# Mamba core units of 32 channels by 4 states, with shared tiles of step sizes and inputs, in a fused attention, FFN and Mamba kernel

## What is computed

```
def step(h, inp):
    dt_t, B_t, C_t, u_t = inp
    dA = jnp.exp(dt_t[..., None] * A)
    h = dA * h + (dt_t * u_t)[..., None] * B_t[:, None, :]
    y_t = jnp.einsum('ben,bn->be', h, C_t)
    return (h, y_t)
```

## Time and profile before

| | |
|---|---|
| median of 3 runs | 813.26 us (810.76 to 814.96) |
| the profiled execution | 808.2 us, its span 806.4 us |
| busy: PE, DVE, ACT, POOL | 729.3, 690.0, 613.8, 598.2 us |
| mean granted TensorE clock | 0.976 of full speed |
| DMA | 152.93 MB, q1 at 70.4% of 16 engines' span |

### The profile page before, as it was taken

How to read it: one execution, slowest core, us unless ns; L and a number is a source line. 1 busy time by engine, 2 the same in 40 slices (tenths; PEclk the granted TensorE clock), 3 DMA queues, 4 the chain that set the end, 5 groups by cost and what they waited for, 6 DMA issues and landing times. The chain is left out here.

```text
span 806.4 us, 22760 instructions
## 1 busy us (share of the span) xinstructions
PE 729.3 (90%) x8284; PEld 441.3 (55%) x8284; DVE 690.0 (86%) x1147; ACT 613.8 (76%) x1227; POOL 598.2 (74%) x589
## 2 busy tenths in 40 slices
PE   6989996998789999999899989979998999788888
PEld 5666653644455446556465366546555555354557
DVE  6878146999999999998899899999998989889963
ACT  4767686899779999998699988888669557656423
POOL 3023254878898998879797798889989989898751
PEclk9999998999999999999999999989999999799999
DMA  6000017798879769877768898979798999799940
GB/s 205 3 3 2 2 57 171 204 232 235 200 210 238 198 190 237 231 220 199 188 201 219 216 251 235 254 204 264 222 246 213 237 259 239 211 284 232 229 118 28
DMA packets 83025, 152.93 MB, mean 190 GB/s; under 512 B 9305, under 2 KB 9954, under 8 KB 82914
## 3 DMA queue, kind: packets, MB, share of 16 engines
q1 hardware_dynamic: 82914, 151.48, 70.4%
HBM read 140.43 MB, written 11.01 MB: 188 GB/s over the span
## 5 line engine op out<-in xcount | busy, mean ns | idle before, releaser
L1798 POOL TENSOR_TENSOR d<-d,cr 128x1024 f32<-128x1024 f32 x128 | 300.4, 2355 | 27.0 <-DVE d L1303 17.3
L1620 ACT ACTIVATE ps<-dt,An 128x512 f32<-128x512 f32 x252 | 170.7, 691 | 59.9 <-DVE d L1303 43.1
L1303 DVE TENSOR_TENSOR_SCAN d<-ps,hl,d 128x512 f32<-128x512 f32 x128 | 157.8, 1266 | 4.4 <-ACT ps L1620 2.6
L1303 DVE TENSOR_TENSOR_SCAN d<-ps,d 128x512 f32<-128x512 f32 x128 | 150.5, 1206 | 6.5 <-ACT ps L1620 4.9
L892 PE MATMUL ps<-h,w 128*128 128x512 f16 (+1 forms) x512 | 118.0, 382 | 7.3 <-DVE h L1238 6.7
L1291 DVE TENSOR_TENSOR d<-ps,d 128x512 f32<-128x512 f32 x182 | 117.3, 671 | 5.9 <-DMA d<-dud 5.9
L1785 POOL TENSOR_TENSOR d<-d,br 128x512 f32<-128x512 f32 x70 | 88.8, 1275 | 19.9 <-DMA d<-dud 16.1
L892 PEld LDWEIGHTS ps<-h,w 128*128 128x128 f16 x512 | 47.6, 99 | 80.9 <-DVE h L1238 17.5
L981 PE MATMUL ps<-d,cst 128*32 128x512 f32 x512 | 69.6, 619 | 7.7 <-POOL d L1798 7.2
L1028 PEld LDWEIGHTS ps<-cst 128*128 128x128 f32 x476 | 59.4, 200 | 18.2 <-issue 10.2
L1028 PE MATMUL ps<-cst 128*128 128x128 f32 x476 | 63.4, 287 | 5.3 <-DMA cst<-in_w 5.3
(11 more groups left out here) (183 smaller groups left out, 1368.8 us busy)
## 6 DMA issues: line engine op xcount, KB each, us to landing
d<-dud SPq DMA_DIRECT2D x252, 256.0 KB, 5.1
dt<-dtd SPq DMA_DIRECT2D x252, 256.0 KB, 5.6
dud<-sE SPq DMA_DIRECT2D x16, 256.0 KB, 4.5
dtd<-sR SPq DMA_DIRECT2D x16, 256.0 KB, 3.9
X<-in_x SPq DMA_DIRECT2D x8, 256.0 KB, 6.2
br<-bcd SPq DMA_DIRECT2D x8, 256.0 KB, 3.3
cr<-bcd SPq DMA_DIRECT2D x8, 256.0 KB, 3.7
out<-X SPq DMA_DIRECT2D x3, 512.0 KB, 5.6
```

Of the source, the lines that this page charges most:

```text
L1303: eng.tensor_tensor_scan(d, banks[u % NG][:, :], d, hl[:, r:r + 1] if m % 2 else 0.0, ALU.mult, ALU.add).then_inc(v_sc, 1)
L1620: eng.activation(banks[u % NG][:, :], src[:, :], ACT.Exp, scale=An[:, g:g + 1]).then_inc(s_da, 1)
L1798: eng.tensor_tensor(d, d, CR[m % 2][:, :].unsqueeze(1).to_broadcast((128, n, 512)), ALU.mult).then_inc(p_cm, n)
```

## The change

A unit becomes 32 channels by 4 states. Unit u of block k = u // 4 has the states 4w to 4w + 3 with w = u % 4, and the four units of a block share their 32 channels. One tile of step sizes and one of inputs then serve four units: `dt4_d` and `du4_d` load 32 rows given 4 times, into 2 slots each (`DT`, and a new `DU`). Since B_t and C_t now differ with w, `BR` and `CR` have four tiles each and are no longer doubled: `br_d` may reload tile w after the last drive that reads it, `cr_d` after the last `out_p`. The roles in the drive are turned round: `bp_s` copies the inputs of a block (`DU`) into `PB`, 62 times instead of 8 times `BR`, and `drive_v` multiplies `PB` by `BR[w]` straight into the slot of `D`, for which it waits itself (`t_y`). `drive_p` reads `DU`. POOL drives the units with w = 0; the first two blocks (`SPREAD`), eight units, are spread by PE. `ND` goes from 12 to 10. `PLACES` has new numbers throughout, and PE's warming products (`WARM`) go from 238 to 207.

```diff
-def channels(r):
-
-    return r // 16, r % 4, r % 16 // 4
-
-
-
-DRIVEN_P = [0, 1, 5, 9, 13, 17, 21, 25, 29]
-
-
-FIRST = 4
+SPREAD = 2
+
+
+DRIVEN_P = [0, 4, 8, 12, 16, 20, 24, 28]
 
 
 def driver(u):
 
-    return "v" if u < FIRST or u % NR not in DRIVEN_P else "p"
+    return "v" if u < 4 * SPREAD or u % NR not in DRIVEN_P else "p"
...
 
-        ND = 12
+        ND = 10
         D = sb("d", [128, ND, 512])
...
-        NT = 6
+        NT, NQ = 2, 2
         DT = sb("dt", [128, NT, 512])
-        BR = [sb(f"br{i}", [128, 512]) for i in range(2)]
-        CR = [sb(f"cr{i}", [128, 512]) for i in range(2)]
+        DU = sb("du", [128, NQ, 512])
+        BR, CR = (sb(n, [128, 4, 512]) for n in ("br", "cr"))
...
-                if m >= 2:
-
-                    eng.wait_ge(t_mo, m - 1)
+
+            def states(m, at):
+
+                return bcd[m % 2][at:at + 4, :].unsqueeze(1).to_broadcast((4, 32, 512))
+
+            def br_d(m, w):
+                u = NR * m - 4 + w
                 eng.wait_ge(l_bc, 16 * (m + 1))
-                for i, dst in enumerate((BR[k], CR[k])):
-                    eng.dma_start(dst[:, :], bcd[k][16 * i:16 * i + 16, :].unsqueeze(1).to_broadcast((16, 8, 512))).then_inc(l_br, 16)
+                if m and driver(u) == "v":
+                    eng.wait_ge(v_dr, driven(u + 1, "v"))
+                elif m:
+                    eng.wait_ge(p_dr, driven(u + 1, "p"))
+                eng.dma_start(BR[:, w, :], states(m, 4 * w)).then_inc(l_b[w], 16)
+
+            def cr_d(m, w):
+                eng.wait_ge(l_bc, 16 * (m + 1))
+                if m:
+                    eng.wait_ge(p_cm, NR * m - 4 + w // 2 * 2 + 2)
+                eng.dma_start(CR[:, w, :], states(m, 16 + 4 * w)).then_inc(l_c[w], 16)
...
-            def rows(src, u):
-
-                m, r = u // NR, u % NR
-                eb, q, w = channels(r)
-                e = 128 * eb + 32 * q + 8 * w
-                return src[m % 2][e:e + 8, :].unsqueeze(0).to_broadcast((16, 8, 512))
-
-            def dt8_d(u):
-                if u >= NT + FIRST:
-                    eng.wait_ge(s_da, u - NT + 1)
-                eng.wait_ge(l_dt, 16 * (u // 16 + 1))
-                eng.dma_start(DT[:, u % NT, :], rows(dtd, u)).then_inc(l_t[u % NT], 16)
-
-            def du8_d(u):
-                if u == FIRST:
-
-                    eng.wait_ge(v_set, V_END)
-                if u >= ND:
-                    eng.wait_ge(t_y, (u - ND) // 4 + 1)
-                eng.wait_ge(l_du, 16 * (u // 16 + 1))
-                eng.dma_start(D[:, u % ND, :], rows(dud, u)).then_inc(l_d[u % ND], 16)
+            def rows(src, k):
+
+                m, eb, q = k // 8, k // 4 % 2, k % 4
+                e = 128 * eb + 32 * q
+                return src[m % 2][e:e + 32, :].unsqueeze(0).to_broadcast((4, 32, 512))
+
+            def dt4_d(k):
+                if k >= NT + SPREAD:
+                    eng.wait_ge(s_da, 4 * (k - NT) + 4)
+                eng.wait_ge(l_dt, 16 * (k // 4 + 1))
+                eng.dma_start(DT[:, k % NT, :], rows(dtd, k)).then_inc(l_t[k % NT], 16)
+
+            def du4_d(k):
+                if k >= NQ + SPREAD:
+                    eng.wait_ge(s_bp, k - NQ - SPREAD + 1)
+                    eng.wait_ge(p_dr, driven(4 * (k - NQ) + 4, "p"))
+                eng.wait_ge(l_du, 16 * (k // 4 + 1))
+                eng.dma_start(DU[:, k % NQ, :], rows(dud, k)).then_inc(l_q[k % NQ], 16)
...
+
+                bank = bank_of["bdt", k] = turn((s_da, 4 * k + 4))
                 eng.wait_ge(v_md, 2)
-                q = slice(32 * u, 32 * u + 32)
+                q = slice(32 * k, 32 * k + 32)
...
-                m, eb, w = k // 8, k // 4 % 2, k % 4
-                if w == 0:
+                m, eb, q = k // 8, k // 4 % 2, k % 4
+                if q == 0:
...
-                for q in range(4):
-                    t = eng.matmul(bank[32 * q:32 * q + 32, :], csel[:, 24 - 8 * w:56 - 8 * w], D[:, (4 * k + q) % ND, :],
+                for w in range(4):
+                    t = eng.matmul(bank[32 * q:32 * q + 32, :], spread[:, 0:32], D[:, (4 * k + w) % ND, :],
                                    start=(w == 0), stop=(w == 3))
...
 
                     eng.wait_ge(l_dt, 16 * n)
                 if n == 1:
-                    eng.wait_ge(t_bdt, FIRST)
+                    eng.wait_ge(t_bdt, SPREAD)
                 eng.wait_ge(p_md, 3 * n + 2)
                 eng.scalar_tensor_tensor(sR[:, :], bank_of["md", m, eb][:, :], 0.0, sL[:, :], ALU.max, ALU.add).then_inc(v_md, 1)
 
             def drive_v(u):
-                m = u // NR
-                d = D[:, u % ND, :]
-                if u < FIRST:
+                m, w, k = u // NR, u % 4, u // 4
+                if u < ND:
 
                     eng.wait_ge(v_set, V_END)
-                    eng.wait_ge(l_br, 32)
-                    eng.wait_ge(t_bdu, u + 1)
-                    eng.tensor_tensor(d, bank_of["bdu", u][:, :], BR[0][:, :], ALU.mult).then_inc(v_dr, 1)
-                    return
-                eng.wait_ge(s_bp, m + 1)
-                eng.wait_ge(l_d[u % ND], 16 * landed(u, ND))
-                eng.tensor_tensor(d, PB[:, :], d, ALU.mult).then_inc(v_dr, 1)
+                else:
+                    eng.wait_ge(t_y, (u - ND) // 4 + 1)
+                eng.wait_ge(l_b[w], 16 * (m + 1))
+                if k < SPREAD:
+                    eng.wait_ge(t_bdu, k + 1)
+                else:
+                    eng.wait_ge(s_bp, k - SPREAD + 1)
+                eng.tensor_tensor(D[:, u % ND, :], PB[:, :], BR[:, w, :], ALU.mult).then_inc(v_dr, 1)
...
-            def bp_s(m):
-
-                if m == 0:
-                    for sm, v in emptied.get(3, ()):
-                        eng.wait_ge(sm, v)
-                else:
-                    eng.wait_ge(v_dr, driven(NR * m, "v"))
-                eng.wait_ge(l_br, 32 * (m + 1))
-                eng.copy(PB[:, :], BR[m % 2][:, :]).then_inc(s_bp, 1)
+            def bp_s(k):
+
+                eng.wait_ge(v_dr, driven(4 * k, "v"))
+                eng.wait_ge(l_q[k % NQ], 16 * landed(k, NQ))
+                eng.copy(PB[:, :], DU[:, k % NQ, :]).then_inc(s_bp, 1)
...
-                    eng.wait_ge(t_bdt, u + 1)
-                    src = bank_of["bdt", u]
+                if k < SPREAD:
+                    eng.wait_ge(t_bdt, k + 1)
+                    src = bank_of["bdt", k]
                 else:
-                    eng.wait_ge(l_t[u % NT], 16 * landed(u, NT))
-                    src = DT[:, u % NT, :]
+                    eng.wait_ge(l_t[k % NT], 16 * landed(k, NT))
+                    src = DT[:, k % NT, :]
                 eng.activation(banks[u % NG][:, :], src[:, :], ACT.Exp, scale=An[:, g:g + 1]).then_inc(s_da, 1)
...
-                m = u // NR
-                d = D[:, u % ND, :]
-                eng.wait_ge(l_br, 32 * (m + 1))
-                eng.wait_ge(l_d[u % ND], 16 * landed(u, ND))
-                eng.tensor_tensor(d, d, BR[m % 2][:, :], ALU.mult).then_inc(p_dr, 1)
+                m, w, k = u // NR, u % 4, u // 4
+                if u < ND:
+                    eng.wait_ge(v_set, V_END)
+                else:
+                    eng.wait_ge(t_y, (u - ND) // 4 + 1)
+                eng.wait_ge(l_b[w], 16 * (m + 1))
+                eng.wait_ge(l_q[k % NQ], 16 * landed(k, NQ))
+                eng.tensor_tensor(D[:, u % ND, :], DU[:, k % NQ, :], BR[:, w, :], ALU.mult).then_inc(p_dr, 1)
...
-                if r == 0:
-                    eng.wait_ge(l_br, 32 * (m + 1))
+                for w in range(u % 4, u % 4 + n):
...
                     eng.wait_ge(p_hl, NR * (m // 2) + r + 2)
-                eng.tensor_tensor(d, d, CR[m % 2][:, :].unsqueeze(1).to_broadcast((128, n, 512)), ALU.mult).then_inc(p_cm, n)
```

More of the change, by code:

```diff
@@ L23 @@
 CONST, NCONST = {}, 0
-for _name, _n in (("ident", 128), ("qmask", 4), ("csel", 56), ("one8", 1), ("rmask", 2), ("spread", 128)):
+for _name, _n in (("ident", 128), ("qmask", 4), ("one8", 1), ("rmask", 2), ("spread", 128)):
     CONST[_name] = (NCONST, _n)
@@ L90, with landed @@
 NCORE = NM * NR
-def channels(r):
-    return r // 16, r % 4, r % 16 // 4
-DRIVEN_P = [0, 1, 5, 9, 13, 17, 21, 25, 29]
-FIRST = 4
+SPREAD = 2
+DRIVEN_P = [0, 4, 8, 12, 16, 20, 24, 28]
 def driver(u):
-    return "v" if u < FIRST or u % NR not in DRIVEN_P else "p"
+    return "v" if u < 4 * SPREAD or u % NR not in DRIVEN_P else "p"
 def driven(u, by):
     return sum(driver(x) == by for x in range(u))
-def landed(u, n):
-    return u // n + 1 - (u % n < FIRST)
+def landed(k, n):
+    return sum(x % n == k % n for x in range(SPREAD, k + 1))
 def rows_of(f):
@@ L155 @@
 FOURS = [(k,) for k in range(NCORE // 4)]
+TILES = [(m, w) for m in range(NM) for w in range(4)]
 STEPS = [
-    (HALVES, 'bp_s mln_p mln_s mln_t mln_v mno_s mxu_s mx_d mx_s mx_t mz_s mz_t silu_s'),
+    (HALVES, 'mln_p mln_s mln_t mln_v mno_s mxu_s mx_d mx_s mx_t mz_s mz_t silu_s'),
     (BLOCKS, 'dr_v dt_d dt_p dt_s dt_t dt_v du_d du_p mu_s mu_t'),
```

(31 more changed lines are left out.)

231 lines of the change are left out of this document (121 added, 110 removed), and 298 rows, old and new, of tables (PLACES, WARM).

## The result

The changed kernel takes 973.96 us in the median (972.53 to 975.16, 4 runs), beside 813.59 us for the kernel before: 1.198 times as long, 95% interval 1.194 to 1.201. The forecast was 850 us, range 800 to 890: the sign was right, and the loss is more than four times the 36 us forecast.

The account below looks back on a forecast made before the run. DVE was taken to bound the kernel: 808.2 us + 5.2 (drives) + 2 (copies) - 9 (waits gone) + 38.5 (late loads) = 845, plus 5.1 from profiled run to median, gave 850 us, range 800 to 890.

Parts of the forecast that it names:

- moved work: Work shifted on other engines: little more on DVE, fewer PE broadcasts and warming products, csum matmuls unchanged; nothing added.
- The loads' term: Loads with outermost size 4 use four DMA engines and come 5.5 us late at seven half starts: +38.5 us.
- in the mean it goes: Per half, the four engines' loads take 62 of 82 us, so on average they keep up.
- the twelve loads: SP's file at a half's start, from a dt to a du; needs 33.8 us on four engines.
- the 11 units of cover: Scans 124 to 134, which DVE can do while a half's first loads arrive: 28.3 us.
- the fifth: The br of w = 3 in the half-start file: lands after 15.6 us, due after some 14; no added delay.
- The landing of the loads: Sign: br and cr land above 5 us after issue with four engines, under 4 with sixteen.
- the gain: DVE's waits behind loads of d and the last decays go: -9 us, bounds 0 and -16.
- Rival 2: Loads spread over sixteen engines, or their delay hidden; every wait behind DMA goes: 804.5 us, faster, chance 0.18.
- Rival 3: Loads harmless as well, but only DVE's direct waits go: 811.5 us, no change, chance 0.11.
- rival 4: ACT becomes the bound with DVE, half of the copies' 31 us reaching the scans: 825 us, slower, chance 0.11.
- Rival 1: Four DMA engines, loads late at each half's start: the forecast itself, own range 836 to 895 us, chance 0.60.

Follow-up runs that it names:

- e1: Changed kernel with a block's four sum matmuls writing four strips of 32 PSUM rows instead of one, sum over state groups left out: 905.24 us.
- e2: Changed kernel with partitions laid out as 4 times channel plus state, so loads go to sixteen DMA engines, not four; still one strip: 911.07 us.
- e3: Changed kernel with both edits, four strips and loads on sixteen DMA engines, sum over state groups left out: 790.64 us.
- e9: Kernel before, a block's four sum matmuls put in one strip and each overwriting it (start and stop at every one) instead of adding: 933.15 us.
- e4: Kernel before with one edit: a block's four sum matmuls write one strip instead of four, mixing channels' sums: 935.0 us.

## Why the prediction was right in sign and far off in size

**The step that failed** is a half sentence under "moved work": "its csum has the same 4 matmuls each", costed at nothing. The count was right and the price was not: +161 us of PE busy, 69 us of time in the changed kernel (e1), 120 where nothing else was late (e2 against e3). The diff showed it: the loop over q became a loop over w while the strip stayed with q. A matmul was costed by its count and form, not by where it writes and what its neighbours write. PE had 62 us to spare in the core, so of 161 more at least 99 had to reach the end. No rival had PE as the bound. That the sign came out right is no luck: with the strip repaired the changed kernel is still 10% to 12% slower (e1).

**The loads' term, +38.5 us: mechanism and place right, size a third.** Four engines: 1737 small packets were forecast for four and 3993 for sixteen; the changed kernel has 1737, e2 and e3 have 3993. The flat two tenths is there. A load takes 2.57 us in the flat stretch (forecast 2.6), which is 0.080 us a packet (taken at 0.081; over the whole page 18.2% of 16 x 972.1 us for 32850 packets is 0.086). The place was right too: of the 111 us by which e1 falls behind e3, 90 are gained at the seven starts, and 15 in scans 12 to 28 of all halves, so "in the mean it goes" nearly holds. What failed is the size of one start: 5.5 us forecast, 12.9 measured (7.3 where PE was the bound as well). The forecast asked only whether the last of the twelve loads comes before the 11 units of cover are used up, and took the fifth as inside the same delay. The traces show waits for earlier ones as well: in half 1 of e1 ACT waits for a du until 217.2 us, DVE for two tiles of br until 222.4 and 225.0, and POOL for cr until 241.6. `DT` and `DU` have two slots, a block's load may start only when the block two before is through, so the loads can't run far ahead. How the 12.9 us add up wasn't worked out. The first half, put at nothing, isn't free either: POOL waits 11.1 and 2.4 us for cr there, and the first scan comes 4.3 us later in e1 than in e3. In all, the late loads cost 115 us with the sum repaired and 63 without.

**Right.** 194 drives at 0.66 us (127.8 for 194, forecast 0.645); 62 copies of 0.59 us, and ACT didn't become the bound: in e3 its copies wait for the drives ahead, while scans wait for decays only 3.0 us there. POOL waits for cr (27.0 us), DVE for br (six times, 14.1 us; once in the first half and at four of the seven starts, where all seven were named), ACT for du above 20 us (24.3). The landing of the loads, named as a sign, can't be read: the view gives none for transfers on four engines.

**Too small was the gain.** Rival 2, sixteen engines and every wait gone, had 804.5 us. e3 is that kernel but for the sum left out, and takes 790.64. DVE's busy time rose by 3.7 us (690.0 to 693.7) and its idle time fell by 21.7 us (116.4 to 94.7), where 16 were allowed. For sT it waited 2.0 us in the core in e3 (10.7 before), for decays 3.0 (7.5 before). Why these too fell wasn't tried by itself.

**The rivals.** Rival 3 and rival 4 fell. Rival 1, the forecast's own, holds as the mechanism of the loads' delay, but not in size: e1, the changed kernel without the strip's price, takes 905.24 us, above the 895 of its range.

## What to carry to other kernels

When a change turns loops round, ask of each matmul with 32 output columns which strip of PSUM partitions its neighbours write: four in a row into one strip take 3.4 times as long as into four, though the trace's mean duration of one record barely moves (608 and 619 ns). Compare busy time by count for each line, also for lines whose count doesn't move. Give a broadcast or tile load an outermost size of 16 or more, by the order of partitions if need be; here 43% of the bytes on a quarter of the engines gained nothing, and a file that was three quarters full in the mean came late wherever many loads fell due together. To learn where a delay arises, compare the start of the same instruction in two traces, one by one. And of two causes that overlap, repairing one shows less than half of what both cost: test them one by one and together.

## What the runs showed of the hardware that wasn't expected

A matmul that overwrites a strip waits for the one before as a summing one does (228.4 and 230.1 us for the 512 records of e9 and e4). Two adjacent blocks in different strips still overlap at their seam: 16 records took 5.37 us where 2 x 3.62 would be 7.24 (changed kernel, at 514.36 us; ends of matmuls are modelled in the trace). The mean granted TensorE clock was 0.922 of full speed in e1_strips, 0.961 in the changed kernel, 0.972 in e3_both and 0.987 in e2_wide. The same 8214 instructions kept PE busy for 756.2 us in e1 and 724.5 in e3. How much of that, and of e1's time, is the clock wasn't split off, so part of the price of the loads may be the clock's.
